# Both halves of a node block together on TensorE: all 128-row work first, then all 64-row work

## What is computed

```python
h = relu(layernorm(x))                       # every node: 64 scalars and 32 vectors of 3 components
skip_s, skip_v = s @ W_skip0, einsum('nmi,mk->nki', v, W_skip1)
s, v = s @ W_nl0, einsum('nmi,mk->nki', v, W_nl1)
# per edge: rows s[dst], v[dst], times weights from a small MLP of edge_attr_64 and the direction of edge_attr_3
agg = segment_sum(tp, src, num_segments=N) / 32
out_s = agg_s @ W_out_s + skip_s             # 96 columns: 64 for silu, 32 for the gate
out_v = einsum('nmi,mk->nki', agg_v, W_out_v) + skip_v
return x + concat([silu(out_s[:, :64]), sigmoid(out_s[:, 64:96])[:, :, None] * out_v])
```

## Time and profile before

| | |
|---|---|
| three runs, median (lowest to highest) | 1210.98 us (1209.78 to 1215.87) |
| the profiled execution: its time, its span | 1209.0 us, 1207.2 us |
| mean granted TensorE clock | 0.958 of full speed |
| TensorE busy, share of the span | 1115.1 us, 92% |
| VectorE busy | 979.8 us, 81% |
| ScalarE busy | 860.4 us, 71% |
| GpSimd busy | 729.7 us, 60% |

### The profile page before, as it was taken

One profiled execution on the slowest core, in us unless ns is written; L12 is line 12 of the kernel. 1 busy time (PEld: TensorE's weight loads), 2 busy tenths in 40 slices (PEclk: granted clock), 3 DMA queues, 4 the chain that ended last, 5 costly groups with the idle time before them and its releaser, 6 DMA issues.

```text
span 1207.2 us, 29282 instructions
## 1 busy us (share of the span) xinstructions
PE 1115.1 (92%) x8847; PEld 939.8 (78%) x8847; DVE 979.8 (81%) x3571; ACT 860.4 (71%) x2069; POOL 729.7 (60%) x860
## 2 busy tenths in 40 slices
PE   6989899999999767889699999999999999999996
PEld 4667788888888656778588788888888788888885
DVE  9999898888886447667488888888888888888874
ACT  0300578877777445566598899899888898889984
POOL 6777587787887777777615544554445544554460
PEclk9999899999999788789599999999999999999999
DMA  9999344444446633444387777777777677777763
GB/s 343 404 403 403 119 131 132 129 131 130 130 129 195 214 104 101 114 113 123 106 296 275 259 286 281 282 255 284 284 282 285 247 286 279 285 265 282 286 214 118
DMA packets 108459, 271.12 MB, mean 225 GB/s; under 512 B 13573, under 2 KB 51751, under 8 KB 108364
## 3 DMA queue, kind: packets, MB, share of 16 engines
q1 hardware_dynamic: 87852, 233.20, 54.9%
q0 software_dynamic: 19200, 36.48, 10.4%
q10 hardware_dynamic: 1312, 0.29, 0.1%
HBM read 126.91 MB, written 143.01 MB: 224 GB/s over the span
## 4 chain that ended last, share of the span: by engine, by line
PE 62%; DVE 12%; POOL 12%; issue 8%; DMA 3%; ACT 2%; SPq 0%; DVEq 0%; POOLq 0%; ACTq 0%
PE bank L1465 16%; PE bank L1478 9%; PE bank L1457 8%; POOL slots L512 7%; PE bank L1469 5%; POOL xg L502 5%; PE bank L1394 4%; PE bank L1297 3%; PE bank L1423 3%; PE bank L1329 3%; DVE ob L1047 2%; PE bank L1411 2%; DVE bin_hot L626 2%; PE bank L1407 2%; PE bank L1409 2%
## 5 line engine op out<-in xcount | busy, mean ns | idle before, releaser
L1246 ACT ACTIVATE nn<-xb,n_bias,n_rstd 128x160 f32<-128x160 f32 x784 | 346.2, 528 | 45.3 <-POOL n_bias L567 40.9
L512 POOL DMA_INDIRECT slots<-msg,sidx x200 | 229.3, 1147 | 75.5 <-issue 56.1
L956 DVE BATCH_NORM_STATS2 n_stat<-xb 128x6 f32<-128x160 f32 x784 | 196.0, 312 | 24.8 <-DMA xb<-x 24.2
L1047 DVE SCALAR_TENSOR_TENSOR ob<-sg,bank 128x128 f32<-128x128 f32 x588 | 131.7, 279 | 72.4 <-ACT ob L1261 70.7
L1478 PE MATMUL bank<-mg,hot 64*128 64x192 f32 x1568 | 171.8, 338 | 7.7 <-DVE hot L1032 7.7
L544 POOL TENSOR_TENSOR n_sum<-n_stat 128x32 f32<-128x32 f32 x24 | 6.9, 287 | 279.5 <-DVE n_stat L956 279.5
L502 POOL DMA_INDIRECT xg<-x,dst_i x136 | 145.7, 1072 | 44.0 <-issue 41.0
L561 POOL TENSOR_TENSOR n_rstd<-n_sum,neg_half 128x8 f32<-128x8 f32 x94 | 160.2, 1704 | 5.7 <-issue 2.9
L1465 PE MATMUL bank<-fwd,nt 128*128 128x160 f32 x784 | 144.6, 307 | 14.3 <-DVE ob L1047 12.4
L1253 ACT ACTIVATE nt<-bank 128x640 f32<-128x640 f32 x196 | 137.5, 702 | 18.1 <-PE bank L1458 14.1
L1054 DVE TENSOR_TENSOR ob<-ob,xb 128x1280 f32<-128x1280 f32 x98 | 146.9, 1499 | 3.4
(11 more groups left out here) (191 smaller groups left out, 2669.9 us busy)
## 6 DMA issues: line engine op xcount, KB each, us to landing
xb<-x SPq DMA_DIRECT2D x97, 640.0 KB, 5.1
out_dram<-ob SPq DMA_DIRECT2D x97, 640.0 KB, 3.3
slots<-blank SPq DMA_DIRECT2D x14, 2744.0 KB
mg<-slots SPq DMA_DIRECT2D x98, 392.0 KB, 4.0
messages<-msg SPq DMA_DIRECT2D x50, 382.8 KB
ef<-edge_feat_t SPq DMA_DIRECT2D x50, 125.0 KB
slots<-msg,sidx POOLq DMA_INDIRECT x200, 4.1
xg<-x,dst_i POOLq DMA_INDIRECT x136, 6.8
```

Of the source, the lines that this page charges most:

```text
L512: pool.indirect_dma_start(slots[:, :], bass.IndirectOffsetOnAxis(ap=sidx[:, m:m + 1], axis=0), msg[:, c, t, 0:MW], None).then_inc(e_sc[c], 16)
L956: done = dve.bn_stats(n_stat[:, u // U, u % U * G + g, :], xb[:, u, g, :])
L1047: last = dve.scalar_tensor_tensor(out=o[:, :, S + V * j:S + V * j + V], in0=sg[:, h, :, :], scalar=1.0, in1=z[:, :, part], op0=ALU.add, op ...
L1246: last = act.activation(nn[:, u % 2, h, spread_of(g % 4)], xb[:, u, g, order_of(g % 4)], ACT.Relu, bias=n_bias[:, u // U, c:c + 1], scale= ...
```

## The change

TensorE's round becomes: the 128-row skip products of both halves, turn(i + 1, 0), then for each half the third component and the messages with 64 rows, then turn(i + 1, 1). `skip` is split for that into `main_part` and `third_part`. ScalarE's round becomes gates and evacuation for half 0, gates and evacuation for half 1, then the norms of both halves of block i + 2. VectorE's round becomes both gates, the one-hots of block i + 1, the residual, and all the statistics of block i + 6. Before the first round, the norms of both halves of blocks 0 and 1, both turns and both evacuations of block 0 are made. The waits are the same ones with their numbers brought in line.

```diff
--- VectorE
                     def round_n(i, u):
-                        if macro_exists(i - 1):
-                            gate(i - 1, before, 1)
-                        if macro_exists(i - 1):
-                            residual(i - 1, before)
-                        if macro_exists(i + 1) and not every:
-                            hot_n(i + 1, after, 0)
-                            hot_n(i + 1, after, 1)
-                        if measure:
-                            stats_n(s, v, 0, 4)
                         gate(i, u, 0)
-                        if measure:
-                            stats_n(s, v, 4, 8)
+                        gate(i, u, 1)
+                        if macro_exists(i + 1) and not every:
+                            hot_n(i + 1, (u + 1) % XU, 0)
+                            hot_n(i + 1, (u + 1) % XU, 1)
+                        residual(i, u)
+                        if macro_exists(s) and macro_exists(i - 2):
+                            stats_n(s, v)
--- ScalarE
                     def evacuate(i, h):
                         act.wait_ge(n.t, 2 * i + h + 1)
-                        wait(act, n.z, 2 * i + h - 1)
+                        wait(act, n.z, 2 * (i - 1) + h + 1)
...
+                    evacuate(0, 1)
                     def round_n(i, u):
-                        if macro_exists(i - 1):
-                            gates(i - 1, (u + 7) % XU, 1)
-                        evacuate(i, 1)
-                        if macro_exists(i + 1):
-                            norm(i + 1, (u + 1) % XU, 1)
-                        gates(i, u, 0)
-                        if macro_exists(i + 1):
-                            evacuate(i + 1, 0)
+                        for h in range(2):
+                            gates(i, u, h)
+                            if macro_exists(i + 1):
+                                evacuate(i + 1, h)
                         if macro_exists(i + 2):
                             norm(i + 2, (u + 2) % XU, 0)
+                            norm(i + 2, (u + 2) % XU, 1)
--- TensorE
                     turn(0, 0, 0)
+                    turn(0, 0, 1)
                     def round_n(i, u):
-                        turn(i, u, 1)
-                        skip(i, 0)
-                        if not every:
-                            add(i, u, 0)
+                        main_part(i, 0)
+                        main_part(i, 1)
                         if macro_exists(i + 1):
                             turn(i + 1, (u + 1) % XU, 0)
-                        skip(i, 1)
+                        for h in range(2):
+                            third_part(h)
+                            if not every:
+                                add(i, u, h)
...
-                            add(i, u, 1)
+                        if macro_exists(i + 1):
+                            turn(i + 1, (u + 1) % XU, 1)
```

More of the change, by code:

```diff
@@ L1106, in round_n @@
                     def round_n(i, u):
-                        before, after = (u + 7) % XU, (u + 1) % XU
                         s, v = i + 6, (u + 6) % XU
-                        measure = macro_exists(s) and macro_exists(i - 2)
-                        if macro_exists(i - 1):
-                            gate(i - 1, before, 1)
-                        if macro_exists(i - 1):
-                            residual(i - 1, before)
-                        if macro_exists(i + 1) and not every:
-                            hot_n(i + 1, after, 0)
-                            hot_n(i + 1, after, 1)
-                        if measure:
-                            stats_n(s, v, 0, 4)
                         if every:
@@ L1121, in round_n @@
                         gate(i, u, 0)
-                        if measure:
-                            stats_n(s, v, 4, 8)
+                        gate(i, u, 1)
[5 more added lines that the diff above has]
+                            stats_n(s, v)
                     macros(dve, round_n)
-                    gate(NM - 1, (NM - 1) % XU, 1)
-                    residual(NM - 1, (NM - 1) % XU)
                 for q in range(NG + 3):
@@ L1263, in nodes @@
                     if OPEN in parts:
-                        norm(0, 0, 0)
-                        norm(0, 0, 1)
-                        norm(1, 1, 0)
+                        for i in range(2):
+                            norm(i, i, 0)
+                            norm(i, i, 1)
                     if ROUNDS not in parts:
@@ L1269, in nodes @@
                     evacuate(0, 0)
+                    evacuate(0, 1)
                     def round_n(i, u):
-                        if macro_exists(i - 1):
-                            gates(i - 1, (u + 7) % XU, 1)
-                        evacuate(i, 1)
-                        if macro_exists(i + 1):
-                            norm(i + 1, (u + 1) % XU, 1)
-                        gates(i, u, 0)
-                        if macro_exists(i + 1):
-                            evacuate(i + 1, 0)
+                        for h in range(2):
+                            gates(i, u, h)
+                            if macro_exists(i + 1):
+                                evacuate(i + 1, h)
                         if macro_exists(i + 2):
                             norm(i + 2, (u + 2) % XU, 0)
+                            norm(i + 2, (u + 2) % XU, 1)
                     macros(act, round_n)
-                    gates(NM - 1, (NM - 1) % XU, 1)
                 for q in range(NG + 3):
@@ L1454, in turn @@
                         pe.wait_ge(n.norm, 2 * i + h + 1)
-                        wait(pe, n.ht, 2 * i + h - 1)
+                        wait(pe, n.ht, 2 * (i - 1) + h + 1)
                         for t in range(4):
@@ L1458, in turn, with main_part @@
                         pe.transpose(q_t[h][:, 4 * P:5 * P], nn[:, u % 2, h, LAST], ident[:]).then_inc(n.t, 1)
-                    def skip(i, h):
-                        z = q_z[h]
+                    def main_part(i, h):
                         pe.wait_ge(n.ht, 2 * i + h + 1)
@@ L1464, in skip, with third_part @@
                         for t in range(4):
-                            pe.matmul(z[:, t, 0:F], nt[:, h, t * P:(t + 1) * P], sides[t // 2][:, skip_cols], start=(t % 2 == 0),
-                                      stop=False, skip_group_check=True)
+                            pe.matmul(q_z[h][:, t, 0:F], nt[:, h, t * P:(t + 1) * P], sides[t // 2][:, skip_cols],
+                                      start=(t % 2 == 0), stop=False, skip_group_check=True)
+                    def third_part(h):
                         for j in range(2):
                             part = slice(HALF * j, HALF * j + HALF)
-                            pe.matmul(z[:, 2 * j:2 * j + 2, F:Z], nt[part, h, 4 * P:5 * P], sides[j][part, skip_z_cols],
+                            pe.matmul(q_z[h][:, 2 * j:2 * j + 2, F:Z], nt[part, h, 4 * P:5 * P], sides[j][part, skip_z_cols],
                                       start=False, stop=every, skip_group_check=True)
@@ L1497, in nodes @@
                     turn(0, 0, 0)
+                    turn(0, 0, 1)
                     def round_n(i, u):
-                        turn(i, u, 1)
-                        skip(i, 0)
-                        if not every:
-                            add(i, u, 0)
+                        main_part(i, 0)
+                        main_part(i, 1)
                         if macro_exists(i + 1):
                             turn(i + 1, (u + 1) % XU, 0)
-                        skip(i, 1)
+                        for h in range(2):
+                            third_part(h)
+                            if not every:
+                                add(i, u, h)
                         if every:
                             add_every(i)
-                        else:
-                            add(i, u, 1)
+                        if macro_exists(i + 1):
+                            turn(i + 1, (u + 1) % XU, 1)
                     macros(pe, round_n)
```

## The result

The changed kernel takes 1299.72 us, median of four runs (1295.85 to 1305.03), against 1212.65 (1209.78 to 1215.87) of the kernel before. The ratio is 1.072, 95% interval 1.066 to 1.078: 7% slower. The forecast was 1313 in a range of 1248 to 1342.

What follows compares the result with a forecast made beforehand. The prediction took TensorE to bound the kernel, with a loop through ScalarE and GpSimd just beneath. Rounds of 6.10 us and the ends gave 1198.4, bias waits added 60.5, clock 51; with 1.8 and 2.0 more, 1313, range 1248 to 1342.

Steps and rivals of the forecast that it cites:

- The loop: Node stage: turn of half 1, evacuation, norm, turn of half 0, third parts and adds take 6.10 us a block.
- TensorE's own 5.51: TensorE's work per block falls from 5.90 to 5.51 us with two of four row changes removed, 38 us in all.
- rival 2: Loop hidden, saving on row changes visible: blocks of 5.51 us; 1150 with bias on time, 1206 with its wait; chance 0.09.
- The wait for the bias: ScalarE waits 2.75 us for GpSimd's bias in 22 groups of four blocks, inside the loop: 60.5 us.
- rival 3: GpSimd's power is held until VectorE's residual ends: bias wait 4.3 us, 34 us more, 1347; chance 0.12.
- The clock: TensorE's idle before late turns halves its clock after eight of nine of 22 gaps, 2.6 us each: 51 us.
- The sum: Whole kernel: 1198.4 with rounds of 6.10, 1258.9 with waits, 1309.9 with clock; 1313 as median.
- Rival 1: Bias waits come as forecast, but TensorE's clock holds or falls seldom: 1263, or 1288 with half the drops; chance 0.27.
- rival 4: VectorE binds: its work with the hole between gates is 5.7 us a block, under 6.10, so no change; no separate chance.

Runs made afterwards that it cites:

- the kernel without both limits: The changed kernel with GpSimd's small operations for two blocks at a time instead of four, and half 0's norm made one round earlier: 1162.96 us, ratio 0.955.
- the first experiment: The changed kernel with the statistics made one block further ahead, for block i + 7 instead of i + 6: 1197.17 us, ratio 0.9905 to the kernel before.
- the third experiment: The changed kernel with statistics one block further ahead, half 0's norm one round earlier, and SyncE's load of x ahead of its other transfers: 1238.54 us, ratio 1.022.

## Why the prediction was right

- **The loop.** Forecast 6.10 us a block, measured 6.04 to 6.05. The step that carried it was that norm(i+2, 0) stands behind evacuate(i+1, 1), and that turn(i+2, 0) needs it. Moving that norm gave 5.68 with the bias in time. TensorE's loss to the loop was forecast as about 0.5 us a block (2.72 - 2.30 = 0.42 by its terms), and is 6.04 - 5.68 = 0.36.
- **TensorE's own 5.51.** This number was wrong, and the prediction's own steps say so: 0.58 + 0.11 + 16 x 0.137 = 2.88 up to turn(i+2, 0) and 2.80 from there on are 5.68, not 5.51. The pair of changes had been priced at 0.39 from the idle of the weight loader; by the steps it is worth 5.90 - 5.68 = 0.22. With the bias on time the old order took 5.90 and the new one, with the norm ahead, 5.68, and the kernels lie 24 us apart. Put back between the products of the two halves the pair cost 0.32 to 0.35, so the price hangs on the place. The forecast was not touched, since its 6.10 came from the path through the norm, which hides this saving; but the saving within reach was 22 us, not 38, and the 1150 and 1206 of rival 2 rest on 5.51. (Nor do these two lie the 60.5 of the wait apart: by the sum the first is 1146.) With 5.68, the kernel without both limits comes to 1202 - 96 x 0.42 = 1162. It took 1163, or 1157 if its ratio of 0.955 is set against the 1211 that the forecast started from.
- **The wait for the bias.** Forecast 22 x 2.75 = 60.5, measured 22 times with a total of 58.4. The chain with its start took 1017.68 - 1013.05 = 4.63 and not 4.9: no small operation started behind a one-hot. The one-hots met only the start of the power, which took 1.69 to 1.78 us in place of 1.66. The residual did not hold the power (rival 3), for in the changed kernel it starts after the power, 0.44 us in the shown group. The lock that rival 3 priced does exist: where the residual was first, seven times in the first experiment and thirteen in the third, the power took 2.7 to 2.9 us. Here is one, of the third experiment:

```profile
906.23 1.49 DVE L1056 TENSOR_TENSOR ob<-ob,xb 128x1280 f32<-128x1280 f32 x1
...
906.33 2.90 POOL L563 TENSOR_TENSOR n_rstd<-n_sum,neg_half 128x8 f32<-128x8 f32 x1
```

- **The clock.** Forecast 51 us for 19.6 spells at 2.6; this is the term that was mis-sized. 19 of 22 gaps were followed by a spell, so the count was right. A stalled round with its successor took about 2.65 us more than without a spell ten times, as forecast, and 1.6 nine times, together about 41, since every second spell lasted 3.4 us and not 6.8. The experiment with the gap filled says as much: 37 by the ratios, and 3.5 for the transposes' own cost.
- **The sum.** From the first add (599.6 in this execution, 594.3 before; the edge stage was later) to the end are 701.6 us against 715.6 in the forecast, 14 less: 2 for the bias, 10 for the clock, 5 for the rounds, and 3 in the other direction that I have not taken apart, in the first and last rounds. The forecast's terms add up to 1313.7, and the median lies 14 us below that too, but by chance: the edge stage, which the change does not touch, ended 5.3 us later than before, and the profiled execution was 3.4 us above the median of its runs, where the forecast had taken it 2.0 below.
- **The rivals.** Rival 1 (the clock holds) was true for three gaps of 22. Rival 2 (saving visible) needed a path 0.45 us shorter; the kernel with the norm ahead has it. VectorE (rival 4) had 0.4 us to spare in a plain round: it sat idle for 0.42 us ahead of the first gate.

## What to carry to other kernels

Before steps of several engines are put in another order, write down for each hand-over how long before its use it is made, in the old order and in the new. Here one norm went from a block ahead of its turn to just in front of it, and closed a loop that was longer than the busiest engine's work. A wait that several blocks share was paid in full once it sat on such a loop, and TensorE paid again with its clock, 41 us on top of some 60; count all deadlines again for each step that is moved, the producers' too, as the third experiment shows. The cure had two parts, the norm a round ahead of its turn and the late bias in smaller portions. And add up TensorE's steps in the new order before a saving is priced: the idle times of the weight loader promised 0.39 us a block, the steps 0.22.

## What the runs showed of the hardware

A gap of 2.8 us in otherwise full work was followed by half clock in 19 of 22 cases, in spells of 6.8 and 3.4 us by turns. With gaps of 2.4 and 2.7 us it was 16 of 22, and the six without a spell were all gaps of 2.4. With throwaway transposes in the gap it was none, and the granted clock was 1.00: the transposes, then, kept it up.

A GpSimd operation of 0.29 us on SBUF took 1.46 us when a VectorE instruction with two SBUF inputs had begun just before it, 22 times out of 22. By the Trainium skill, SBUF — State Buffer, section Who interferes with whom, such a pair contends for a shared read interface under an exclusive lock, and the order of issue decides which of the two is blocked. The trace agrees where GpSimd comes second, for the small operations and for the power (2.7 to 2.9 us behind a residual). It does not agree where VectorE comes second. In the changed kernel 22 residuals began while a power still had 1.26 us to run, and took 1.48 us, as the others did. The power beside them took 1.69 to 1.78 us. One of them:

```profile
1015.35 1.70 POOL L561 TENSOR_TENSOR n_rstd<-n_sum,neg_half 128x8 f32<-128x8 f32 x1 [0.16 <-POOL n_sum L554]
...
1015.79 1.48 DVE L1054 TENSOR_TENSOR ob<-ob,xb 128x1280 f32<-128x1280 f32 x1
```
